# Between two chunks of a recurrent layer: weighted rows one slab pair ahead, two sets of transfers on other queues, a filler product of 256 columns

## What is computed

```python
def loss_fn(params, kk, vv):
    pred = _mlp(params, kk)                 # silu(k (W0 + P0)) (W1 + P1)
    return jnp.mean((pred - vv) ** 2)

def step(carry, xs):
    cp, cm = carry
    k_t, v_t, q_t, a_t, th_t, e_t = xs
    g = jax.vmap(jax.grad(loss_fn))(cp, k_t, v_t)
    s = lambda c: c[:, :, None]
    nm = jax.tree_util.tree_map(lambda m, gg: m * s(e_t) - s(th_t) * gg, cm, g)
    np_ = jax.tree_util.tree_map(lambda p, m: p * (1.0 - s(a_t)) + m, cp, nm)
    out_t = jax.vmap(_mlp, in_axes=(0, 0))(np_, q_t)
    return (jax.lax.stop_gradient((np_, nm)), out_t)

_, ys = jax.lax.scan(step, (cur_p, cur_m), xs)   # 248 steps, 64 sequences, D = 64, hidden 256
```

## Time and profile before

| | us |
|---|---|
| median of 3 runs | 10781.32 |
| the three runs | 10769.77, 10781.32, 10793.72 |
| span of the profiled execution | 10794.5 |
| recurrent layer in it | about 2815 to 9760 |
| TensorE busy, share of the span | 9005.6, 83% |
| VectorE, ScalarE, Pool busy | 4911.9, 2097.8, 227.2 |

### The profile page before, as it was taken

How to read it: one execution, slowest core, us unless ns; L and a number is a source line. 1 busy time by engine, 2 the same in 40 slices (tenths; PEclk the granted TensorE clock), 3 DMA queues, 4 the chain that set the end, 5 groups by cost and what they waited for, 6 DMA issues and landing times. The chain is left out here.

```text
span 10794.5 us, 373142 instructions
## 1 busy us (share of the span) xinstructions
PE 9005.6 (83%) x152370; PEld 5786.4 (54%) x152370; DVE 4911.9 (46%) x13031; ACT 2097.8 (19%) x4839; POOL 227.2 (2%) x184
## 2 busy tenths in 40 slices
PE   6799953424699999999999999999999999967777
PEld 2466631122466676666666766667667666642222
DVE  3444435446634444444344444443443444445555
ACT  0233321221111111111111111111111111113343
POOL 0000000001100000000000000000000000000000
PEclk8799975557899999999999999999999999988888
DMA  2000001425311121211111211222222222200000
GB/s 61 8 11 11 11 22 39 137 41 105 85 30 55 54 57 53 56 55 55 56 55 52 57 54 56 79 74 82 69 75 81 73 76 77 61 19 12 12 9 11
DMA packets 961796, 563.30 MB, mean 52 GB/s; under 512 B 376334, under 2 KB 956694, under 8 KB 959766
## 3 DMA queue, kind: packets, MB, share of 16 engines
q1 hardware_dynamic: 947990, 544.62, 18.7%
q0 software_dynamic: 13312, 12.57, 0.6%
HBM read 331.63 MB, written 188.08 MB: 48 GB/s over the span
## 5 line engine op out<-in xcount | busy, mean ns | idle before, releaser
L2387 PE MATMUL bank<-mv,hdiag 128*32 128x144 f32 x63744 | 2052.5, 286 | 11.2 <-DVE hdiag L2580 9.5
L2387 PEld LDWEIGHTS bank<-mv,hdiag 128*32 128x32 f32 x63744 | 1933.5, 110 | 85.8 <-DVE hdiag L2580 12.5
L2440 PE MATMUL bank<-mvt,ydiag 128*32 128x256 f32 x31872 | 1942.6, 381 | 0.0
L2440 PEld LDWEIGHTS bank<-mvt,ydiag 128*32 128x32 f32 x31872 | 1038.1, 110 | 568.8 <-issue 1.0
L2289 PE MATMUL bank<-yth,r_ident 128*128 128x512 f32 x896 | 507.9, 678 | 119.3 <-ACT mv L2232 58.8
L2243 ACT ACTIVATE work<-work 128x128 f32<-128x128 f32 x498 | 154.3, 310 | 2223.1 <-DVE work L2570 2223.1
L431 PE MATMUL att_bank<-att_qa,att_ka 32*124 32x248 f32 x2048 | 583.0, 411 | 0.5 <-DVE att_qa L645 0.5
L421 PE MATMUL att_bank<-att_ka,att_qn 32*124 32x496 f32 x1024 | 577.0, 661 | 3.7 <-DVE att_mx L606 3.7
L606 DVE TENSOR_REDUCE att_mx<-att_bank 124x2 f32<-124x496 f32 x512 | 344.9, 675 | 491.1 <-PE att_bank L421 491.1
L2613 DVE TENSOR_TENSOR rep<-bank,ta 128x128 f32<-128x128 f32 x249 | 72.7, 292 | 997.2 <-PE bank L2387 997.2
L2232 ACT ACTIVATE mv<-bank 128x256 f32<-128x256 f32 x1024 | 313.1, 388 | 836.6 <-PE bank L2321 836.5
(11 more groups left out here) (416 smaller groups left out, 11379.5 us busy)
## 6 DMA issues: line engine op xcount, KB each, us to landing
ring<-between_slopes SPq DMA_DIRECT2D x320, 512.0 KB, 4.1
baset<-between_base_old SPq DMA_DIRECT2D x265, 128.0 KB, 2.1
baset<-between_base SPq DMA_DIRECT2D x265, 128.0 KB, 2.2
between_base<-work SPq DMA_DIRECT2D x256, 128.0 KB
hist<-h SPq DMA_DIRECT2D x1992, 8.0 KB
hist<-y SPq DMA_DIRECT2D x1992, 2.0 KB
hist<-dl SPq DMA_DIRECT2D x1992, 8.0 KB
between_base_old<-bo SPq DMA_DIRECT2D x240, 128.0 KB
```

The costliest lines, as they stand in the source:

```text
L2387: mm = e.matmul(psP[32 * j:32 * j + 32, 0:MW], hdiag[:, hf, r, j, :], mv1[:, hf, r, j, :], start=(hf == 0 and r == 0), stop=(hf == 1 and r ...
L2440: mm = e.matmul(psBack[hf][32 * j:32 * j + 32, :], ydiag[:, n, j, :], both, start=(n == 0), stop=(n == 7))
```

## The change

There are four edits:

1. VectorE computes `wy` of the next pair inside slab X (X even), between its `sa` and `sb` operations; the first is computed ahead of the loop. The names in the list `vec_u`, from which the counts come, move with it. The wait for nw(X-3) goes, since the loop's wait for nw(X) contains it.
2. The eight `cc` loads are issued by ACT at the head of its chunk, after a wait for VectorE.
3. The eight slope stores are issued by Pool, between its first clearing and the cc product, with the wait for the last `dl`. The first chunk is written out ahead of the loop, without the waits for a chunk before it.
4. The filler in `turned` has 256 columns. Those at the head and the end of the update keep 512.

VectorE also waits for `alt` before the first step of a chunk.

```diff
--- before.py
+++ after.py
@@ -1928,8 +1928,10 @@
 
         ends = [f"{a}{X}{k}" for X in range(16) for a in ("sa", "sb", "sn") for k in range(2)]
         vec_u = ["tabz", "tabe", "taba", "tabd", "tabo", "ut", "uc", "fix1", "fix2", "wt", "wc"]
+        vec_u += ["wy0"]
         for X in range(16):
-            vec_u += ([f"wy{X // 2}"] if X % 2 == 0 else []) + [f"{a}{X}{k}" for a in ("sa", "sb", "sn") for k in range(2)]
+            vec_u += [f"sa{X}0", f"sa{X}1"] + ([f"wy{X // 2 + 1}"] if X % 2 == 0 and X < 14 else [])
+            vec_u += [f"{a}{X}{k}" for a in ("sb", "sn") for k in range(2)]
         vec_u += ["rep0", "rep1", "x0", "cm", "cmx", "d3a", "d3b", "d3c", "cu0", "cu1"]
         vec_s = ["om", "sp", "adiag", "both", "grep", "y1", "gdiag", "y2", "y", "ydiag", "xb", "drep", "xb2", "ddiag",
                  "dh1a", "dh2a", "dh3a", "da", "xa", "ha", "hd0", "dh1", "dh2", "dh3", "d", "xz", "h"]
@@ -1969,6 +1971,7 @@
             q.base = 0
         s_set, s_own = sem("set_dma"), sem("settled")
         s_own_pe = sem("settled_pe")
+        s_own_act = sem("settled_act")
         s_pool = sem("pool_set")
         s_pe = sem("settled_tensor")
         s_v = sem("vec_set")
@@ -2118,12 +2121,19 @@
         with nc.Block() as block:
             @block.gpsimd
             def _(e):
-                with e.Fori(0, NCH) as c:
-
-                    for q in (V, T, A):
-                        e.wait_ge(q.sem, q.begun(c))
+                def chunk(c, first=False):
+                    if not first:
+                        for q in (V, T, A):
+                            e.wait_ge(q.sem, q.begun(c))
+                            settled(e, s_own_pe)
+                    e.memset(spare[:, 512:1024 + 2 * TN], 0.0).then_inc(P.sem, 1)
+                    if not first:
+                        e.wait_ge(hist_d.sem, c * (hist_d.unit * CH))
                         settled(e, s_own_pe)
-                    e.memset(spare[:, 512:1024 + 2 * TN], 0.0).then_inc(P.sem, 1)
+                    for m in range(2):
+                        for j in range(4):
+                            dst = DXD[bass.ds(c * CH, CH), 16 * j + 8 * m:16 * j + 8 * m + 8, :].rearrange("t b f -> b t f")
+                            e.dma_start(dst, hist[:, m * 4 + j, HD + D:]).then_inc(slopes_out.sem, 16)
                     e.wait_ge(cc_in.sem, cc_in.upd(c, "in"))
                     settled(e, s_own_pe)
                     rows = ccp[:, 0:16 * CH].rearrange("p (q t) -> p q t", t=CH)
@@ -2132,6 +2142,10 @@
                     e.wait_ge(T.sem, T.upd(c, "nw15"))
                     settled(e, s_own_pe)
                     e.memset(spare[:, 0:1024 + 4 * TN], 0.0).then_inc(P.sem, 1)
+
+                chunk(0, first=True)
+                with e.Fori(1, NCH) as c:
+                    chunk(c)
 
             @block.sync
             def _(e):
@@ -2151,16 +2165,6 @@
                         for i in range(8):
                             src = CT[bass.ds(c, 1), bass.ds(48 + c * CH, CH), :, :].rearrange("a s (m i) f -> s (a m) i f", m=2)[:, :, i, :]
                             e.dma_start(ctn[16 * i:16 * i + 16, i % 2, :, :], src).then_inc(ctn_in.sem, 16)
-                    for i in range(8):
-
-                        src = CT[bass.ds(c, 1), bass.ds(64 + c * CH, CH), :, :].rearrange("a s (m i) f -> s (a m) i f", m=2)[:, :, i, :]
-                        e.dma_start(ccp[16 * i:16 * i + 16, 0:16 * CH].rearrange("p (m f) -> p m f", m=2), src).then_inc(cc_in.sem, 16)
-                    e.wait_ge(hist_d.sem, c * (hist_d.unit * CH))
-                    settled(e, s_own)
-                    for m in range(2):
-                        for j in range(4):
-                            dst = DXD[bass.ds(c * CH, CH), 16 * j + 8 * m:16 * j + 8 * m + 8, :].rearrange("t b f -> b t f")
-                            e.dma_start(dst, hist[:, m * 4 + j, HD + D:]).then_inc(slopes_out.sem, 16)
                     for q in range(8):
                         row = CT[bass.ds(c, 1), bass.ds(64 + c * CH, 1), 0:1, :].rearrange("a s g f -> (a s g) f")
                         src = bass.AP(row.tensor, row.offset + (16 * q + 1), [[128, 16], [2049, CH - 1], [1, 1]])
@@ -2222,6 +2226,12 @@
                 e.preload_act_table(ACT.Sigmoid)
 
                 def chunk(c, steps):
+
+                    e.wait_ge(V.sem, V.begun(c))
+                    settled(e, s_own_act)
+                    for i in range(8):
+                        src = CT[bass.ds(c, 1), bass.ds(64 + c * CH, CH), :, :].rearrange("a s (m i) f -> s (a m) i f", m=2)[:, :, i, :]
+                        e.dma_start(ccp[16 * i:16 * i + 16, 0:16 * CH].rearrange("p (m f) -> p m f", m=2), src).then_inc(cc_in.sem, 16)
                     for X in range(16):
                         for k in range(2):
                             j, m, g, n = slab(X, k)
@@ -2283,10 +2293,10 @@
                 def chunk(c, steps, part):
                     ahead_part = part if part < len(PARTS) else None
 
-                    def kept_warm(out, n):
+                    def kept_warm(out, n, cols=512):
 
                         for _ in range(n):
-                            e.matmul(out, ident[:, :], yth[:, :, :].rearrange("p a s -> p (a s)"), start=True, stop=True)
+                            e.matmul(out[:, 0:cols], ident[:, :], yth[:, :, :].rearrange("p a s -> p (a s)")[:, 0:cols], start=True, stop=True)
 
                     def new_terms(X):
 
@@ -2311,7 +2321,7 @@
                             if X:
                                 e.wait_ge(A.sem, A.upd(c, f"c{X - 1}{k}1"))
                             if k == 0:
-                                kept_warm(psC[k], 1)
+                                kept_warm(psC[k], 1, 256)
                         for k in range(2):
                             j, m, g, n = slab(X, k)
                             e.wait_ge(V.sem, V.upd(c, f"sn{X}{k}"))
@@ -2513,18 +2523,18 @@
                     own(V.upd(c, "wt"))
                     go(e.tensor_copy(WC.rearrange("p t s -> p s t"), WT[:, :, :]), "wc")
 
+                    def weighed(G):
+                        j, m = G // 2, G % 2
+                        go(e.tensor_tensor(wy[:, G % 2, :, :, :],
+                                           hist[:, m * 4 + j, HD:HD + D].unsqueeze(1).unsqueeze(1).to_broadcast([128, 2, 2, D]),
+                                           cmx[:, :, j, m, :].unsqueeze(3).to_broadcast([128, 2, 2, D]), ALU.mult), f"wy{G}")
+
                     e.wait_ge(T.sem, T.begun(c))
+                    e.wait_ge(hist_y.sem, c * (hist_y.unit * CH))
+                    weighed(0)
                     for X in range(16):
                         G = X // 2
                         j, m = G // 2, G % 2
-                        if X % 2 == 0:
-                            if X == 0:
-                                e.wait_ge(hist_y.sem, c * (hist_y.unit * CH))
-                            if X >= 4:
-                                e.wait_ge(T.sem, T.upd(c, f"nw{X - 3}"))
-                            go(e.tensor_tensor(wy[:, G % 2, :, :, :],
-                                               hist[:, m * 4 + j, HD:HD + D].unsqueeze(1).unsqueeze(1).to_broadcast([128, 2, 2, D]),
-                                               cmx[:, :, j, m, :].unsqueeze(3).to_broadcast([128, 2, 2, D]), ALU.mult), f"wy{G}")
                         e.wait_ge(T.sem, T.upd(c, f"nw{X}"))
                         both = []
                         for k in range(2):
@@ -2534,6 +2544,8 @@
                         for t, ps, ca, cb, ce in both:
                             go(e.scalar_tensor_tensor(out=t[:, 0:HD], in0=t[:, 0:HD], scalar=ca, in1=ps[:, 0:HD],
                                                       op0=ALU.mult, op1=ALU.add), "sa")
+                        if X % 2 == 0 and X < 14:
+                            weighed(G + 1)
                         for k, (t, ps, ca, cb, ce) in enumerate(both):
                             own(V.upd(c, f"sa{X}{k}"))
                             go(e.scalar_tensor_tensor(out=t[:, 0:HD], in0=t[:, HD:], scalar=cb, in1=t[:, 0:HD],
@@ -2579,6 +2591,7 @@
                         e.wait_ge(P.sem, P.upd(c, "hz"))
                         nm(e.tensor_copy(diag_h(0), turned_h(0)))
 
+                    e.wait_ge(al_in.sem, al_in.upd(c, "in"))
                     own(V.upd(c, "cu1"))
                     e.engine_nop().then_inc(V.sem, V.gap("xa"))
                     onward(0, 0)
```

## The result

The changed kernel takes 10530.54 us (median of 4 runs, 10528.3 to 10542.56), the kernel before 10787.52 beside it (10769.77 to 10797.1). The ratio is 0.9768, with a 95% interval of 0.9754 to 0.9782. A later measurement of the same kernel on another chip gave 10541.86 against 10770.23, a ratio of 0.9789 (0.9774 to 0.9804).

A forecast was written before the change was run, and what follows sets the result against it. Losses in the update between chunks: TensorE idling, slow products behind it, and unread fillers. Savings 98 + 56 + 86 + 48 + 3 = 291 us, less 11 for clock and 8 for late transfers, 272: 10509 us, range 10480 to 10600.

The forecast's parts named there:

- The total at full clock: The 16 update stretches, first product of new terms to second clearing: 983.9 us falls to 16 x 43.3, 291 us less.
- 3 of update 0, which no part names: Item of 3 us within the 291 us saving, placed in update 0 and covered by no part.
- The clock term: TensorE's clock at the update's start: 48 us gained if it holds, 11 us off for falls in one update of four.
- 2.1 lies nearer to the first: TensorE's 2.1 us idling ahead of slab 0 likened to 1.72 us without slow products, rather than 2.77 us with them.
- the first slow stretch stays: Rival: slow products after the wait for slab 0 in every update, 45 us lost instead of 11, 10543 us; chance 0.25.
- fillers: Fillers between slabs cut to 256 columns: 14 x 0.44 = 6.1 us per update, 98 us in all.
- weighted rows: Weighted rows computed early on VectorE, so TensorE no longer waits: 3.5 us per update, 56 us in all.
- two transfers: Coefficient loads and slope stores off SP's queue, so ACT's wait for base stores goes: 86 us.
- Cost 0: The moved transfers delay nothing: ACT's eight loads take 6.4 us, Pool's eight stores 12.2 us, both covered by slack.
- SP's queue stays late: Rival: ACT's and SP's issues exclude each other, base stores 4.9 us back, 75 us lost in all, 10584 us; chance 0.10.
- The rival of 5.6 us: Rival: VectorE and TensorE hand over badly, 5.6 us per steady pair, 54 us lost in all, 10563 us; chance 0.14.
- The slower case: Rival: clock stays at 1.2 GHz through the update because halved fillers leave TensorE too little work, +285 us, 11066 us; chance 0.03.

The follow-up runs named there:

- e6: Changed kernel with four more 256-column fillers ahead of slab 0's turned block and Pool's coefficient product behind its second clearing: 10492.0 us, ratio 0.9744.
- After: The changed kernel with all four edits, against the kernel before: 10530.5 us, ratio 0.9768.
- e5: Changed kernel with four more 256-column fillers ahead of slab 0's turned block, nothing else: 10490.1 us, ratio 0.9748.
- e12: Changed kernel with the wait ahead of slab 0 filled, Pool's coefficient product later, and 128-column fillers in slabs 2 to 14: 10463.4 us, ratio 0.9719.
- e13: Changed kernel with Pool's coefficient product later and no fillers in the slabs but five ahead of slab 0's turned block: 10451.8 us, ratio 0.9706.
- e1: Changed kernel with the slabs' filler back at 512 columns, nothing else: 10613.3 us, ratio 0.9858.
- after_again: The changed kernel, unchanged, measured again on another chip: 10541.9 us, ratio 0.9789.
- e3: Changed kernel with coefficient loads and slope stores both back on SP's queue ahead of the base stores: 10653.0 us, ratio 0.9891.
- e6b: Changed kernel with Pool's coefficient product moved behind its second clearing, nothing else: 10513.4 us, ratio 0.9776.
- e10: Changed kernel with the coefficient loads back on SP's queue and the slope stores left on Pool: 10543.8 us, ratio 0.9799.
- e7: Changed kernel with the slabs' filler cut from 256 to 128 columns, nothing else: 10583.9 us, ratio 0.9838.
- e2: Changed kernel with the weighted rows made late again, at the head of each even slab on VectorE: 10639.5 us, ratio 0.9872.
- e4: Kernel before with only the filler cut to 256 columns: 10729.9 us, ratio 0.9973.

## Why the prediction was right, and where it was not

**The total at full clock held.** The forecast had 16 x 43.3 = 692.8 us for the stretches, 291 less than before. e6, in which nothing but the clock and the late starts differs, has 697.5, 286.4 less. Of the 4.7 us between the two sums 3.4 are "3 of update 0, which no part names": update 0 needs 46.74 us at full clock, so that item was never there to save. The steady pair (5.12 forecast) is 5.13, the turned blocks stand within 0.1 us of their forecast times.

**The clock term was mis-sized, and it is the whole miss in the updates.** The forecast took 11 us for a fall in one update of four, and 8 for late stores. After loses 748.6 - 697.5 = 51.1 us to slow products and late starts, and nothing to stores. The step that failed is "2.1 lies nearer to the first": from one idle time of 1.72 us with no fall and one of 2.77 with a fall I read that idling of 2.1 would mostly be harmless. The wait came out at 1.83 us, nearer still, and the clock fell all the same. The row that I compared with was no match: ahead of the eight fillers, idle times of 1.72 to 1.82 us occur 42 times in all 14 profiles, and in none is the clock low while the fillers run; of the 168 of 2.3 to 3.3 us there, 101 show it. Behind one filler, ahead of the first turned block, the same length brings it mostly. So the idle time alone doesn't tell; what stands around it counts too. Counted there, with no slow product ahead of TensorE's next wait for ACT as "clock kept":

| idle, us | kernels | updates | clock kept |
|---|---|---|---|
| up to 1.11 | e5, e6, e12, e13 | 64 | 64 |
| 1.40 to 1.42 | e1 | 10 | 9 |
| 1.83 to 1.84 | after, after_again, e3, e6b, e10 | 71 | 18 |
| 1.87 to 2.8 | after, after_again, e1 | 15 | 0 |

(In e13 two updates have slow products in the last slab, behind another wait of 1.27 us; they cost nothing ahead of the clearing. In e7, with its shorter fillers, 2 of 16 stay fast behind 2.4 and 2.6 us, so the table is no law. Before, e2 and e4 are not in it: there a second wait, of 2.0 us for the weighted rows, follows one of 1.07 to 2.5, and all 48 updates fall.) What decides within the 71 stays open. The rival "the first slow stretch stays" is what happened in 13 updates: at 3.9 us per fallen update (51.1 / 13) it cost more than the 2.8 it was priced at (some of it is the late starts, below). Its 10543 us is nearer to the measured time than the forecast is.

**Why the time came so near.** In the updates the forecast wanted 272 us and got 235.3. A further 12.2, 11.8 and 4.3 us went where no line changed, within what profiles of this program differ by (table at the top). The near hit of the total is partly this luck; the size of the miss in its own place is 36.7 us. On the other chip, after_again takes 228 us less than before, with 239 less in its updates.

**The parts don't add as they were told.** By the sums:

| edit | forecast | alone on before | taken out of after |
|---|---|---|---|
| fillers | 98 | 43.4 | 65.1 |
| weighted rows | 56 | not run | 107.6 |
| two transfers | 86 | not run | 124.4 |

Taken out one by one the three come to 297 us, together they brought 235.3. The forecast's 291 was a difference of two timetables, and so right; its split gave the fillers what only fillers and rows together bring: a steady pair is 7.01 us with neither, 6.59 with the short fillers (e4, e2), 5.98 with the early rows (e1) and 5.13 with both, so 0.42 and 1.03 alone and 1.88 together. Likewise the transfers: on the old queue the base stores start at t = 23.3 to 23.8 in update 6 however soon the slabs get there, so what the other edits save ahead of them is waited off (94.8 us of waiting in e3, 53.8 in before).

**The queues.** "Cost 0" for ACT and Pool holds, with two corrections. ACT's eight took 6.77 us in update 6 for 6.4 forecast. Pool's took 4.75 for 12.2: the row of 1,528 ns that I took is of another kind of transfer, and the lower end, 6.6, was the nearer. Because Pool is done at t = 2, its coefficient product comes at t = 2 and not behind t = 9 (13.2 in before), and so meets VectorE's operations for slab 0: the early weighting, or the sb behind it. The forecast named that product only as queued on Pool. In each update with a late start, of all kernels, the product begins at t = 1.7 to 3.3. Four updates of after start 0.5 to 0.9 us late for it. The rival "SP's queue stays late" is out: SP issued eight dl stores in 5.06 us (4.91 in before) while ACT issued eight loads in 6.77, from 5307.07 to 5314.3. 16 issues in 7.2 us is 0.45 each, less than the 0.61 that one takes on SP alone. The Trainium skill's "Perfetto Trace Analysis" (DMA Instruction — HWDGE) has the descriptor generator locked by one sequencer at a time; here the two don't exclude each other for the length of an issue, and a lock held for a part of it can't be told from these rows. How much they slow each other is small: the median issue of these loads is 0.59 us on ACT and 0.56 on SP in before, and the 0.85 of ACT's in update 6 stand beside the 0.80 of SP's, alone, in the earlier trace rows.

**VectorE and TensorE** hand over without loss: 5.13 us a pair, no idling. VectorE's own pace is 5.05 with a weighting (e13), forecast 5.13. The rival of 5.6 us is out.

**The slower case**, low clock through the update, did not come, but its reason did where the change goes further: with 128 columns and the gap left open the products were slow for up to 44 us. e12 and e13 show that the steady part doesn't lose the clock for want of fillers: with the gap filled the same work and less holds 1.00. The Trainium skill ("TensorE: Matmul & The Clock Gate", The HAM clock gate) describes the full clock as something that activity must win; here that fits the return (slow in e7, with its short fillers), while whether it falls at all changed with the idle time ahead of slab 0 (e5, e6, e12, e13: 64 of 64 updates kept it).

## What to carry to other kernels

Price a set of edits as the difference of two timetables, and don't hand shares of it to single edits: here one edit alone brought 0.3% and the three 2.3%. A filler that keeps the clock belongs into the idle time: here five in the gap brought 50 us (with the later product), and those of the other slabs, once the gap was filled, only cost 40. With the gap open they were worth having: there, shortening them from 256 to 128 columns cost 53 to 75 us. A kernel with the gap open and no fillers was not run. When a step is moved away from a busy queue, ask also what it now meets at its new time; the moved stores were free, but the product queued behind them came 11 us sooner than before and met VectorE.
